# A second tile of each even chunk picked by TensorE from one-hots, in place of a gather by GpSimd

## The reference

```python
# layer 0
z = (B[:, :, None] * xj[:, None, :]).reshape(Etot, S * C)    # xj = x[src], B: 8 spline weights per edge
msg = z @ W.reshape(S * C, C)
agg = segment_sum(msg, dst)
out = agg / max(cnt, 1) + x @ root        # then batch norm, ELU, residual, layer norm
# layer 1
msg = x1[src] + edge_attr_64
agg = segment_sum(msg, dst)
h = relu(agg @ W1 + b1) @ W2 + b2         # then batch norm, residual, layer norm
```

## Time and profile before

| | us |
|---|---|
| median of 3 runs | 596.18 |
| lowest, highest | 589.14, 597.19 |
| profiled execution, its own time | 601.57 |
| its span, first to last instruction | 599.8 |
| PE busy | 508.7 |
| DVE busy | 407.5 |
| POOL busy | 375.2 |
| ACT busy | 367.9 |

### The profile page before, as it was taken

One profiled execution on the slowest core, in us unless ns is written; L12 is line 12 of the kernel. 1 busy time (PEld: TensorE's weight loads), 2 busy tenths in 40 slices (PEclk: granted clock), 3 DMA queues, 4 the chain that ended last, 5 costly groups with the idle time before them and its releaser, 6 DMA issues.

```text
span 599.8 us, 13973 instructions
## 1 busy us (share of the span) xinstructions
PE 508.7 (85%) x4151; PEld 407.9 (68%) x4151; DVE 407.5 (68%) x1624; ACT 367.9 (61%) x662; POOL 375.2 (63%) x382
## 2 busy tenths in 40 slices
PE   4269998997797998896997898797997998799993
PEld 2258877876686877685886777686886887344532
DVE  6996885875755676575675666476476554879875
ACT  7575995885867786685785777674242232450054
POOL 6777777777777777777777777777777760000000
PEclk9998997998989998898898989799575556699997
DMA  7633553544535344345343445352244110000002
GB/s 144 140 87 74 120 117 78 124 111 109 126 78 118 89 109 111 89 106 118 72 118 100 104 108 119 71 119 64 45 96 75 25 25 3 0 1 1 1 2 53
DMA packets 89144, 48.75 MB, mean 81 GB/s; under 512 B 76252, under 2 KB 77667, under 8 KB 89069
## 3 DMA queue, kind: packets, MB, share of 16 engines
q1 hardware_dynamic: 75949, 35.40, 24.9%
q0 software_dynamic: 11968, 12.28, 10.9%
q10 hardware_dynamic: 1152, 0.16, 0.2%
HBM read 46.86 MB, written 0.93 MB: 80 GB/s over the span
## 4 chain that ended last, share of the span: by engine, by line
PE 50%; POOL 19%; DMA 11%; DVE 8%; issue 8%; ACT 2%; DVEq 0%; SPq 0%; POOLq 0%; ACTq 0%
POOL rows L529 19%; PE ps L681 11%; DMA rows<-in_x,idx 10%; PE ps L640 9%; PE ps L600 8%; PE ps L860 6%; PE ps L625 5%; PE ps L865 2%; PE ps L619 2%; DVE pair L1298 1%; PE ps L608 1%; PE ps L715 1%; PE ps L893 1%; PE ps L589 1%; PE ps L630 1%
## 5 line engine op out<-in xcount | busy, mean ns | idle before, releaser
L529 POOL DMA_INDIRECT rows<-in_x,idx x374 | 373.9, 1000 | 116.2 <-issue 101.8
L681 PE MATMUL ps<-whot_room,rows 128*128 128x96 f32 x816 | 183.3, 311 | 44.8 <-DMA rows<-in_x,idx 43.0
L681 PEld LDWEIGHTS ps<-whot_room,rows 128*128 128x128 f32 x816 | 145.1, 220 | 57.2 <-issue 37.1
L1001 ACT CAST adj<-ps 125x500 f32 x208 | 122.9, 591 | 89.3 <-PE ps L608 76.3
L988 ACT ACTIVATE u<-u,own 128x768 uint8<-128x768 uint8 (+1 forms) x168 | 152.5, 958 | 28.5 <-DMA u<-codes_scratch 28.5
L600 PE MATMUL ps<-pair,ohp 128*125 128x300 bf16 (+1 forms) x416 | 151.3, 366 | 14.4 <-DVE ohp L1302 8.9
L1298 DVE TENSOR_SCALAR pair<-iota_h,comb 128x300 bf16<-128x300 int16 (+1 forms) x416 | 104.1, 313 | 62.0 <-PE ps L608 60.3
L640 PE MATMUL ps<-xs,u 125*128 125x192 bf16 x1050 | 138.1, 258 | 2.6 <-issue 1.5
L1302 DVE TENSOR_SCALAR ohp<-iota_h,srcp 128x125 bf16<-128x125 int16 x416 | 108.4, 273 | 1.3 <-issue 1.3
L640 PEld LDWEIGHTS ps<-xs,u 125*128 125x128 fp8e4 x1050 | 96.1, 106 | 13.0 <-issue 3.5
L1313 DVE TENSOR_TENSOR agg<-agg,ps 128x24 f32 x416 | 75.6, 182 | 35.7 <-PE ps L625 29.9
(11 more groups left out here) (209 smaller groups left out, 381.6 us busy)
## 6 DMA issues: line engine op xcount, KB each, us to landing
u<-codes_scratch SPq DMA_DIRECT2D x42, 400.0 KB, 4.2
rows<-in_edge_attr SPq DMA_DIRECT2D x51, 256.0 KB
rows<-in_x,idx POOLq DMA_INDIRECT x374
x_now<-in_x SPq DMA_DIRECT2D x25, 31.2 KB
adj<-in_x SPq DMA_DIRECT2D x1, 700.0 KB
xs<-in_x SPq DMA_DIRECT2D x1, 700.0 KB
out<-u SPq DMA_DIRECT2D x3, 224.0 KB
adj<-in_edge_attr SPq DMA_DIRECT2D x1, 576.0 KB
```

Source lines behind the costliest of these rows:

```text
L529: pool.indirect_dma_start(rows[:, s, t, 0:C], None, x, bass.IndirectOffsetOnAxis(ap=idx[:, at:at + 1], axis=0)).then_inc(gathered[0][0] if ...
L681: last = nc.tensor.matmul(z_ps[:, half, at:at + ZW], rows[:, s, t, :], whot[:, par, t, :], start=True, stop=True)
L1001: nc.scalar.copy(bass.AP(adj, offset=start, ap=[[NT * NA, PN], [NA, NT], [1, GWIN]]), m_ps[0:PN, bank_of(phase, g), 0:PAIRS].rearrange("p ...
```

## The change

In the 20 even chunks from 6 to 44 PE picks a second tile, tile 6 (`TAKEN - 1`), and POOL gathers 6 tiles there in place of 7. A third buffer, `more_codes`, holds the codes of these tiles; 20 rows are added to the table of codes. SP loads a row into it (`load_more`), and DVE, not ACT, makes the one-hots, with five comparisons over 640 bytes each against the partition's own code (`make_more`), behind the weights of each odd chunk. All picks share the one PSUM bank. In an even chunk PE picks tile 7 of the next chunk at positions 1 to 3 (25 matmuls) and begins the second tile of the chunk after it at positions 5 and 6 (12); in the odd chunk it ends that tile at positions 1 to 3 (13) and picks tile 7 at positions 5 and 6 (25). DVE empties the bank at the matching places (`keep_taken` in the first half of even chunks, `keep_more` in the first half of odd ones). Beside that, some semaphores are merged with others and a marker, `begun`, is removed.

```diff
-    SHARES = {t: range(NT * (t - 1) // 6, NT * t // 6) for t in range(1, 7)}
+    MORE_FROM = TAKE_FROM + 3
+    MORES = (TAKE_TO - MORE_FROM + 1) // 2
+    ROWS = TAKES + MORES
+    MORE_SPLIT = NT // 2
...
+    def is_more(c):
+        return MORE_FROM <= c < TAKE_TO and c % STEP == 0
...
+    def shares_of(c):
+        if c % STEP == 0 and is_more(c + 2):
+            return spread_over(range(NT), range(1, 4)), spread_over(range(MORE_SPLIT), range(5, 7))
+        if c % STEP == 1 and is_more(c + 1):
+            return spread_over(range(NT), range(5, 7)), spread_over(range(MORE_SPLIT, NT), range(1, 4))
+        return spread_over(range(NT), range(1, 7)), {}
+
+    MORE_PIECES = [range(j, j + 5) for j in range(0, NT, 5)]
...
+        more_codes = sb("more_codes", [P, HOTS], U8)
+        more_hots = more_codes[0:PN, :].bitcast(F8)
...
+            def load_more(n):
+                if n > 0:
+                    sp.wait_ge(more_taken, n)
+                sp.dma_start(more_codes[:, :], codes_dram[TAKES + n:TAKES + n + 1, :].to_broadcast([P, HOTS])
+                             ).then_inc(more_loaded, 16)
...
                 if s % STEP == 0:
                     load_x(i * (SLOTS // STEP) + (s // STEP - 1))
+                if is_more(c):
+                    load_more((c - MORE_FROM) // STEP)
                 if taken_too:
                     sp.wait_ge(taken, c - TAKE_FROM)
-                    sp.sem_inc(begun, 1)
                     load_codes(c, s % 2)
...
-                for t in range(TAKEN if one_taken else CH):
+                for t in range(CH - takes_of(c)):
...
+            def take_more(n, js):
+                if js[0] == 0:
+                    pe.wait_ge(more_ready, n + 1)
+                    pe.wait_ge(taken_kept, MORE_FROM + n * STEP - TAKE_FROM)
+                for j in js:
+                    last = nc.tensor.matmul(taken_ps, more_hots[:, j * P:(j + 1) * P], xs[0:PN, j, :],
+                                            start=(j == 0), stop=(j == NT - 1))
+                if js[-1] == NT - 1:
+                    last.then_inc(more_taken, 1)
...
+            def make_more(n):
+                dve.wait_ge(more_loaded, n * 16 + 16)
+                for js in MORE_PIECES:
+                    of = more_codes[:, js.start * P:js.stop * P]
+                    last = nc.vector.tensor_scalar(of, of, own_code[:, 0:1], None, ALU.is_equal)
+                last.then_inc(more_ready, 1)
+
+            def keep_more(c):
+                n = (c - MORE_FROM) // STEP
+                dve.wait_ge(more_taken, n + 1)
+                nc.vector.tensor_reduce(
+                    rows[:, c % SLOTS, TAKEN - 1, 0:C], taken_ps.rearrange("p (n c) -> p c n", n=PARTS), AX.X, ALU.add
+                    ).then_inc(more_kept, 1)
...
                     dve.wait_ge(m_ready, c * GPC + (GPC // 2 + 1))
+                    if is_more(c + 1):
+                        keep_more(c + 1)
+                    if takes and is_more(c + 2):
+                        keep_taken(i, par)
                     build_pairs(after, par, 0)
...
                     dve.wait_ge(m_ready, c * GPC + (GPC + 1))
-                    if takes:
+                    if takes and not is_more(c + 2):
                         keep_taken(i, par)
                     build_pairs(after, par, 1)
...
                     build_weights(after, par)
+                    if is_more(c + 3):
+                        make_more((c + 3 - MORE_FROM) // STEP)
```

More of the change, by code:

```diff
@@ L172, in gnn_two_layers @@
         hots = [u[0:PN, N - (2 - b) * (HOTS // 4):N - (1 - b) * (HOTS // 4)].bitcast(F8) for b in range(2)]
-        made = z_room[0:TAKES, :]
+        made = z_room[0:ROWS, :]
         src_taken = made[:, HOTS // 4:HOTS // 4 + P].bitcast(I32)
         made = made[:, 0:HOTS // 4].bitcast(U8)
-        above = whot_room[0:TAKES, :].bitcast(I16)
+        above = whot_room[0:ROWS, :].bitcast(I16)
+        more_codes = sb("more_codes", [P, HOTS], U8)
+        more_hots = more_codes[0:PN, :].bitcast(F8)
+        own_code = sb("own_code", [P, 1])
         tile_starts = sb("tile_starts", [P, NT])
@@ L467, in _ @@
             sp.wait_ge(taken, TAKES + 1)
+            sp.wait_ge(more_taken, MORES)
             sp.wait_ge(taken_kept, TAKES)
@@ L534, in _ @@
             for c in range(SLOTS):
-                gather_chunk(0, c, in_step=False, one_taken=(c >= TAKE_FROM))
+                gather_chunk(0, c, in_step=False)
             for c in range(SLOTS, NCH):
-                gather_chunk(c // AHEAD, c % AHEAD, last=(c == NCH - 1), one_taken=(c < TAKE_TO))
+                gather_chunk(c // AHEAD, c % AHEAD, last=(c == NCH - 1))
             def gather_again(of, layer):
@@ L669, in chunk @@
                     half = t // (CH // 2)
-                    if takes_next and t in SHARES:
-                        take_rows(i * SLOTS + (s + 1), prev, t)
+                    if takes_next and t in shares:
+                        take_rows(c + 1, prev, shares[t])
+                    if takes_next and t in more_shares:
+                        take_more((c + 2 - par - MORE_FROM) // STEP, more_shares[t])
                     if t == 0:
@@ L675, in chunk @@
                     if t % (CH // 2) == 0:
-                        pe.wait_ge(gathered[s][half], second_half(i, c, s) if half else i * GATHERED + GATHERED)
+                        pe.wait_ge(gathered[s][half], second_half(c, s) if half else i * GATHERED + GATHERED)
                         pe.wait_ge(zsb_ready, c * 2 + (half + 1))
+                    if is_more(c) and t == TAKEN - 1:
+                        pe.wait_ge(more_kept, (c - MORE_FROM) // STEP + 1)
                     if one_taken and t == TAKEN:
@@ L774, in last_chunk @@
                     else:
-                        pe.wait_ge(gathered[s][1], second_half(i, c - SLOTS, s) + STEP * 16)
+                        pe.wait_ge(gathered[s][1], second_half(c - SLOTS, s) + STEP * 16)
                     products(ts, 1 - n)
@@ L963, in _ @@
                 last = nc.scalar.activation(above[:, j * P:(j + 1) * P], src_taken, ACT.Relu,
-                                            bias=tile_starts[0:TAKES, j:j + 1])
+                                            bias=tile_starts[0:ROWS, j:j + 1])
             last.then_inc(prepared, 1)
             act.wait_ge(prepared, ABOVE)
-            nc.scalar.activation(made, above, ACT.Relu, scale=-1.0, bias=top[0:TAKES, 0:1]).then_inc(prepared, 1)
+            nc.scalar.activation(made, above, ACT.Relu, scale=-1.0, bias=top[0:ROWS, 0:1]).then_inc(prepared, 1)
             act.wait_ge(prepared, CODES)
```

64 lines of the change are left out of this document (34 added, 30 removed).

## The result

The changed kernel takes 589.41 us (median of 20 runs, 583.62 to 595.07) against 596.12 us for the kernel before (20 runs): 6.7 us less, ratio 0.9876 (95% interval 0.985 to 0.9902). The forecast was 18.4 us less. The profiled execution took 589.67 us, span 587.6 us.

The account below looks back on a forecast made before the run. GpSimd's gathers were taken to bound the loop. Removed gathers 25.9 us, less 5.5 for contention and 2 for the near tie with TensorE, save 18.4 us: 578 us from the 596.18 median, range 569 to 600.

Parts of the forecast that it names:

- The 25.9 us for 20 gathers: GpSimd's queue: 20 even chunks lose one gather each at 1.294 us, 25.9 us saved.
- the multiply's law: GpSimd: a gather starting under a VectorE instruction waits its rest less 0.13 us; 0.14 us each, 5.5 us in all.
- My upper bound of 13 us for contention: GpSimd: 0.34 us for each of 1.9 gathers starting within a 2.5 us run of comparisons, 20 times.
- I leave that loss in: TensorE, two early chunks: 7.1 us lost to ACT and VectorE's checks, kept unchanged in the sum.
- the wait at position 5: Even chunks: TensorE waits 0.1 us for VectorE to empty the picks' bank; 0 or 1.6 us at the extremes.
- the pair: Two chunks on TensorE: 14.12 us at full clock plus 2.1 for 25 picks plus 0.1 wait, 16.35 us.
- The tie: Chunk 44's end: TensorE at 402 us against GpSimd at 405, nearly equal; 2 us taken off the saving.
- Rival 1: TensorE becomes the bound, three chunks at half clock, gain about 6 us: 590 us; chance 0.21.
- Rival 2: The whole gain, no contention and no tie, 25.9 us: 570 us; chance 0.05.
- rival 3: VectorE's run, at 4.0 us, makes TensorE late at position 5 in each pair: 612 us; chance 0.15.
- Rival 4: Ports shut VectorE out: each comparison gets in only between two gathers, 6.25 us a run: 646 us; chance 0.04.
- After the last gather nothing changes: Kernel's end: after the last gather, at 491.93 us before the change, no change was expected.

Follow-up runs that it names:

- second pair of profiles: The kernel before and the changed kernel each profiled once more, unchanged: 599.89 us and 593.83 us, one run each.
- more picks: Changed kernel with the first pick of each chunk's own tile made five or nine times: 588.25 us (0.9837) and 589.18 us (0.9896).
- ten comparisons: Changed kernel with ten byte comparisons of two or three blocks in place of five of five blocks: 583.57 us (0.9777).
- late start: Changed kernel with the second tile from chunk 12 on instead of 6, so 357 gathers: 585.69 us (0.9797).
- before-with-comparisons: Kernel before plus only the third loads of codes and the byte comparisons, all 374 gathers, no second picks: 603.15 us (1.0109).
- no comparisons: Changed kernel without VectorE's five byte comparisons; third codes still loaded, second tile picked with zeros: 577.98 us (0.9701).

## Why the prediction was wrong, step by step

**The bound** was right: GpSimd's gathers set the end before and after, but for the few us behind the last gather.

**GpSimd, the failed step.** The 25.9 us for 20 gathers hold (24.9 at the plain pitch). The price of the new comparisons, 5.5 us by the multiply's law, came out at 5.9, partly by luck: 25 gathers were held 0.24 us each, where the price stood for 39 at 0.14. In the second profile it is 7.3 us. What failed is that the sum priced contention only where the change adds an instruction, and kept the old multiply's as it stood. It rose by 9.1 us (10.3 in the second pair of profiles). So "GpSimd's part is then 25.9 - 5.5 = 20.4 us, between 13 and 26" measured 9.4, or 7.0 in the second pair. My upper bound of 13 us for contention did not include this, since it too covered the new run alone.

Why it rose: a held gather, its neighbours and their pauses fill 8.26 us, and so does a chunk of the changed kernel. Before, TensorE waited for gathers and its chunks varied, so the multiplies met gathers at all offsets. The more picks show that another pace undoes the rise, with the same multiplies and comparisons; the ten comparisons (14.4 us, a pair of 16.7) fit it. That the early lateness is what makes the loop even (it gives GpSimd a lead of three chunks at chunk 12, where it was one before, so TensorE never pauses until the lead is used up) fits the late start, where TensorE waits for rows again from 180 us on and the holds are at 15.9; by itself this is only argued.

**TensorE, the second failed step.** "I leave that loss in": I took the early chunks' 7.1 us as a constant. But the run of comparisons goes directly ahead of VectorE's checks, in front of the reduction that TensorE now waits for at position 5: 2.65 us of run and 2.9 of checks delay the reduction to 91.69, and TensorE waits 3.69 us. It waits as long again at 111.95 for ScalarE, which had itself waited 6.09 us for VectorE's last check. Chunk 8 is 13 us later; what each wait has in that is not taken apart. That the comparisons among the checks are the cause is shown from both sides: before-with-comparisons ends chunk 8 at 116.6 (there TensorE waits 4.09 us for the old reduction), no comparisons at 104.0, late start at 104.8. The price on GpSimd's queue was small in itself, a stop of 2.55 us, since GpSimd may be up to three chunks ahead.

**The terms that held.** VectorE's run was put at 2.5 us and takes 2.65; the wait at position 5, put at 0.1 us a pair, is 1.3 us in all in the 11 pairs between 150 and 330 us (0.4 for the bank, 0.9 for the one-hots); the pair was put at 16.35 us and takes 16.28; the clock was to exceed 0.91 and is 0.96; 354 gathers, 0.30 us apart. Three readings were off without weight in the sum: the chunk read at 391.58 us is chunk 41, an odd one (before, both kinds carry the same work); under the multiply the trace before has 36 gathers of 1.25 us between 60 and 440 us, not 33 of 1.28; and 0.14 us for 1.94 gathers in 20 runs is 5.4. The Trainium skill, "VectorE: DVE Perf Modes", The TRN2 errata, gave an estimate of 0.39 us for a comparison; the trace disagrees, with 0.54 at least and 0.546 in the median.

**The tie** (-2 us) did not occur at chunk 44: from 150 to 330 us TensorE is even and at full clock. What TensorE did cost the queue, 2.25 us, it cost in the early chunks; that this is near the 2 us is luck.

**The rivals.** Rival 1 named 590 us, and 589.4 came, but not by its mechanism: the clock is 1.00 throughout from 150 to 330 us, and TensorE's work can shrink or grow without moving the time. Rival 2 fell with the 36.6 us that gathers are held, rival 3 with the run at 2.65 us. Rival 4 fell too: VectorE is not shut out, and loses 0.25 us a run in 17 of the 20 runs (2.65 us for 2.40). Its rule, the Trainium skill, "SBUF — State Buffer", Who interferes with whom, says of VectorE in a two-port mode that whoever issues first holds the shared ports for the whole instruction; the trace disagrees for these comparisons: the 40 that lie wholly under a gather take 0.54 to 0.55 us, no more than the shortest. Nor does the gather that starts at 217.59 hold the multiply that starts 0.15 us later and takes 0.94.

**The base.** I took the saving off the median, though it was worked out in an execution 5.4 us above it. By profiled executions the change saves 11.9 us (601.57 to 589.67), in the second pair 6.1, by medians 6.7. By spans the 12.2 us of the first pair are 9.4 at the last gather and 3.1 in the stretch behind it, less 0.4 behind that; so "After the last gather nothing changes" held for the work and not for the clock, and the first pair of profiles shows the change 3 us better than its queue. What sets an execution of the kernel before at 589 or at 601 us is not settled here; the same sum without comparisons (25.9 - 2) would have given 572, and 578 was measured.

## What to carry to other kernels

When two engines hold each other up, price the contention of the whole loop after a change, not that of the added instruction: a change of pace alone moved 8 us of it here (23.5 to 15.7), and cutting VectorE's long instructions into pieces took 10 to 15 us off under the multiply. A step that is put into a loop also lands in the loop's first rounds, among one-off work: look there for what it queues behind. And an engine that is busy all the time can still be beside the path: add work to it and see, and look at what else moved, since two effects may cancel. The best versions here start the second tile at chunk 12 with the multiply in four (0.9708), and with ten comparisons as well (0.9693); their intervals overlap.

## What the runs showed of the hardware

A gather and the multiply hold each other one way only: a gather that starts 0.22 us into the multiply takes 1.55 us in place of 0.94, while the 19 multiplies that start during a gather take 0.94 to 0.96 us. With comparisons the hold goes both ways. In 17 of the 20 runs of byte comparisons one comparison, in which a gather ends, takes 0.75 us in place of 0.55, and the run takes 2.65 us. In the other three no comparison is longer, the run takes 2.40, and the gathers that start in it are held longer instead (1.32 to 1.42 us in place of 1.11):

```profile
160.90 2.40 DVE L1402 TENSOR_SCALAR more_codes<-more_codes,own_code 128x640 uint8<-128x640 uint8 x5
...
161.07 1.42 POOL L558 DMA_INDIRECT rows<-in_x,idx  x1 [0.30 <-issue]
162.79 1.42 POOL L558 DMA_INDIRECT rows<-in_x,idx  x1 [0.30 <-issue]
```

How long the instruction is matters more than that there is one: five comparisons of 640 bytes hold 5.9 us, ten of half that size 0.4. And 70 gathers that start under VectorE's 16-bit comparisons of 125 values (0.25 us each) are held 0.3 us in all; of these comparisons, the 79 that fall wholly into the pause between two gathers take 0.37 us on average.
